# Layer norm statistics of a four-layer graph network: the eps addition and the shift on GpSimd beside the power

## The reference

```
def _layernorm(x, axis=-1, eps=1e-05):
    m = jnp.mean(x, axis=axis, keepdims=True)
    v = jnp.var(x, axis=axis, keepdims=True)
    return (x - m) / jnp.sqrt(v + eps)

x = _layernorm(x + _L0_gnn_ref(x, adj, weight, bias))      # (adj x + x) W + b, each row over its length
x = _layernorm(x + _L1_gnn_ref(x, adj, adj, ..., 5))       # five steps of a gated recurrent unit
x = _layernorm(x + _L2_gnn_ref(x, adj, W, b))              # normalized adjacency, then a linear map
x = _layernorm(x + _L3_gnn_ref(x, adj, W, e, bias))        # attention over adj > 0, softmax, two maps
```

## Time and profile before

| | us |
|---|---|
| median of 3 runs | 800.88 (800.42 to 801.36) |
| the profiled execution | 799.98 |
| its span, first to last instruction | 798.3 |
| PE busy | 770.0 (96%) |
| DVE busy | 651.3 (82%) |
| ACT busy | 515.2 (65%) |
| POOL busy | 117.1 (15%) |

### The profile page before, as it was taken

How to read it: one execution, slowest core, us unless ns; L and a number is a source line. 1 busy time by engine, 2 the same in 40 slices (tenths; PEclk the granted TensorE clock), 3 DMA queues, 4 the chain that set the end, 5 groups by cost and what they waited for, 6 DMA issues and landing times.

```text
span 798.3 us, 12062 instructions
## 1 busy us (share of the span) xinstructions
PE 770.0 (96%) x3822; PEld 638.7 (80%) x3824; DVE 651.3 (82%) x1578; ACT 515.2 (65%) x1050; POOL 117.1 (15%) x127
## 2 busy tenths in 40 slices
PE   7999988899999999999999999999999999999996
PEld 6888766687888888888888888888877787888885
DVE  6788999988877777777778777777999999986444
ACT  4768756678666666666666666666677766665445
POOL 1354422200000000000000000000112133332222
PEclk9999999999999999999999999999999999999998
DMA  6300000100100000000000000000000000000112
GB/s 186 128 1 2 1 0 1 53 1 9 45 1 0 1 1 0 0 0 0 0 0 0 0 0 0 0 1 1 1 1 1 1 2 1 1 0 14 53 54 93
DMA packets 8782, 13.09 MB, mean 16 GB/s; under 512 B 2336, under 2 KB 3872, under 8 KB 8480
## 3 DMA queue, kind: packets, MB, share of 16 engines
q1 hardware_dynamic: 8736, 12.53, 4.6%
HBM read 7.28 MB, written 5.24 MB: 16 GB/s over the span
## 4 chain that ended last, share of the span: by engine, by line
PE 67%; DVE 24%; ACT 5%; issue 2%; DMA 1%; SPq 0%; POOL 0%; ACTq 0%
PE agg_ps L930 11%; PE agg_ps L932 11%; PE agg_ps L931 11%; PE gate_ps L860 5%; PE gate_ps L862 5%; PE gate_ps L861 5%; PE cand_ps L860 3%; PE cand_ps L862 3%; DVE stats L765 3%; PE cand_ps L861 3%; PE turn_ps L969 3%; PE gate_ps L867 3%; PE cand_ps L867 3%; DVE nat_lo L777 2%; DVE cand L733 2%
## 5 line engine op out<-in xcount | busy, mean ns | idle before, releaser
L576 POOL TENSOR_TENSOR rstd<-mean_var,half 128x4 f32<-128x4 f32 x64 | 78.5, 1226 | 570.6 <-DVE mean_var L772 570.5
L930 PE MATMUL agg_ps<-adj_hi,nat_hi 128*128 128x512 f32 x384 | 151.9, 396 | 0.0
L932 PE MATMUL agg_ps<-adj_hi,nat_lo 128*128 128x512 f32 x384 | 150.1, 391 | 0.0
L931 PE MATMUL agg_ps<-adj_lo,nat_hi 128*128 128x512 f32 x384 | 149.6, 390 | 0.0
L462 ACT ACTIVATE reset_hi<-gate_r 128x512 fp32r<-128x512 f32 x80 | 50.6, 632 | 105.2 <-DVE gate_r L741 105.2
L724 DVE TENSOR_TENSOR agg_lo<-agg_ps,agg_hi 128x512 fp32r<-128x512 f32 x80 | 55.1, 689 | 63.6 <-ACT agg_hi L429 63.5
L390 ACT ACTIVATE res<-res,shift,rstd 128x128 f32<-128x128 f32 x210 | 87.9, 484 | 10.1 <-DVE shift L784 10.1
L932 PEld LDWEIGHTS agg_ps<-adj_hi,nat_lo 128*128 128x128 f32 x384 | 72.0, 188 | 16.1
L931 PEld LDWEIGHTS agg_ps<-adj_lo,nat_hi 128*128 128x128 f32 x384 | 72.2, 188 | 15.6
L930 PEld LDWEIGHTS agg_ps<-adj_hi,nat_hi 128*128 128x128 f32 x384 | 72.2, 188 | 15.0
L446 ACT ACTIVATE gate_r<-gate_ps,bias 128x512 f32<-128x512 f32 x80 | 55.1, 689 | 39.4 <-PE gate_ps L862 39.4
(11 more groups left out here) (174 smaller groups left out, 1705.6 us busy)
## 6 DMA issues: line engine op xcount, KB each, us to landing
res<-in_x SPq DMA_DIRECT2D x16, 256.0 KB, 5.5
out<-res SPq DMA_DIRECT2D x16, 256.0 KB, 2.0
rows<-in_adj SPq DMA_DIRECT2D x4, 256.0 KB, 3.9
mix_rows<-feat SPq DMA_DIRECT2D x1, 1024.0 KB, 3.9
later<-mix_rows SPq DMA_DIRECT2D x1, 1024.0 KB, 4.8
gate_z<-in_L_gnn_w_w SPq DMA_DIRECT2D x3, 128.0 KB, 5.4
gate_r<-in_L_gnn_bias SPq DMA_DIRECT2D x2, 64.0 KB, 5.5
gate_z<-in_L_gnn_u_w SPq DMA_DIRECT2D x2, 64.0 KB, 4.6
```

The source lines that it names most:

```text
L576: pool.tensor_tensor(rstd[:, i % RING, :], mean_var[:, i % RING, :, 1], half[:, :], ALU.pow).then_inc(rstd_made, 1)
L930: pe.matmul(ps, nat_hi[:, b, k, :], m_hi[:, k, :], start=(k == 0), stop=False)
L931: pe.matmul(ps, nat_hi[:, b, k, :], m_lo[:, k, :], start=False, stop=False)
L932: last = pe.matmul(ps, nat_lo[:, b, k, :], m_hi[:, k, :], start=False, stop=(k == T - 1))
```

## The change

VectorE no longer adds eps and no longer makes the shift. GpSimd waits for `aggregated` instead of `stats_made` and does four operations on 128 x 4 elements: `shift = -mean`, `var + eps` in place, the power into `rstd`, and, behind a wait for its own power, `shift * rstd`. The first two each go through `link`, which makes GpSimd wait for its own operation. The shift is made in the slot of the statistics, no longer a slot later, and `rstd_made` and `shift_made` both come from GpSimd.

```
--- before.py
+++ after.py
@@ -294,7 +294,7 @@
         state_hi_made = sem("state_hi_made")
         squared, length_made, shift_made = sem("squared"), sem("length_made"), sem("shift_made")
         statted, aggregated = sem("statted"), sem("aggregated")
-        stats_made, rstd_made = sem("stats_made"), sem("rstd_made")
+        rstd_made = sem("rstd_made")
         normed, normed_act = sem("normed"), sem("normed_act")
         split_hi_made, split_lo_made = sem("split_hi_made"), sem("split_lo_made")
         l2_hi_made, l2_lo_made, mix_hi_made = sem("l2_hi_made"), sem("l2_lo_made"), sem("mix_hi_made")
@@ -572,9 +572,14 @@
                         pool.tensor_tensor(r, r, half[:, :], ALU.pow).then_inc(length_made, 1)
                 for n in norms_at(s, "stats"):
                     i = NORMED.index(n)
-                    pool.wait_ge(stats_made, i + 1)
-                    pool.tensor_tensor(rstd[:, i % RING, :], mean_var[:, i % RING, :, 1], half[:, :],
-                                       ALU.pow).then_inc(rstd_made, 1)
+                    pool.wait_ge(aggregated, i + 1)
+                    r = mean_var[:, i % RING, :, 1]
+                    back = shift[:, i % RING, :]
+                    link(pool.tensor_scalar(back, mean_var[:, i % RING, :, 0], -1.0, None, ALU.mult))
+                    link(pool.tensor_scalar(r, r, EPS_LN, None, ALU.add))
+                    pool.tensor_tensor(rstd[:, i % RING, :], r, half[:, :], ALU.pow).then_inc(rstd_made, 1)
+                    pool.wait_ge(rstd_made, i + 1)
+                    pool.tensor_tensor(back, back, rstd[:, i % RING, :], ALU.mult).then_inc(shift_made, 1)
                 k = s - L2_ROWS_AT
                 if 0 <= k < T:
                     pool.wait_ge(turn_read, reads(TURN_NO["d_row", 0]))
@@ -768,9 +773,6 @@
                     for t in range(T):
                         last = dve.bn_aggr(mean_var[:, i % RING, t, :], stats[:, i % 4, t, :])
                     last.then_inc(aggregated, 1)
-                    dve.wait_ge(aggregated, i + 1)
-                    dve.tensor_scalar(mean_var[:, i % RING, :, 1], mean_var[:, i % RING, :, 1], EPS_LN, None,
-                                      ALU.add).then_inc(stats_made, 1)
                 for n in norms_at(s, "split"):
                     if stage(n) != L3:
                         dve.wait_ge(split_hi_made, nth(SPLIT, n))
@@ -778,11 +780,6 @@
                                           nat_hi[:, n % B, :, :].bitcast(F32), ALU.subtract).then_inc(split_lo_made, 1)
                 if s + 3 < B:
                     x_lo(s + 3)
-                for n in norms_at(s, "shift"):
-                    i = NORMED.index(n)
-                    dve.wait_ge(rstd_made, i + 1)
-                    dve.scalar_tensor_tensor(out=shift[:, i % RING, :], in0=mean_var[:, i % RING, :, 0], scalar=-1.0,
-                                             in1=rstd[:, i % RING, :], op0=ALU.mult, op1=ALU.mult).then_inc(shift_made, 1)
                 k = s - ADJ_AT
                 if 0 <= k < T:
                     dve.wait_ge(adj_hi_made, k + 1)
```

More of the change, by code:

```diff
@@ L780, in slot @@
                     x_lo(s + 3)
[L781 to L785, removed]
                 k = s - ADJ_AT
```

## The result

The changed kernel takes 794.61 us (median of 4 runs, 794.53 to 795.43) against 800.65 us (800.22 to 801.36) for the kernel before beside it: ratio 0.9926, 95% interval 0.9909 to 0.9943, 6.04 us less. The profiled execution took 795.43 us with a span of 793.7 us. The forecast was 794.4 us. The total fits; two of its terms don't, and they miss in opposite directions.

What follows compares the result with a forecast made beforehand. VectorE was taken to set the pace only in two stretches, with TensorE holding most of the rest. Terms -1.9 - 4.7 + 0 + 0.1 = -6.5 us, applied to the 800.88 us median, gave 794.4 us; range 790.5 to 799.5.

Steps and rivals of the forecast that it cites:

- Step 1: Eps add and shift removed from VectorE: 0.19 plus 0.07 us, together 0.26 us less per norm.
- Step 2, stretch A: Layer 0's norms overlapping the first recurrent step, slots 16 to 23: seven slots pay 0.265 us each, 1.9 us.
- step 6: GpSimd's 512-wide operations in eight slots start about 1.0 us later and meet other VectorE operations: -4.8 to +1.8 us, taken as zero.
- Step 2, stretch B: Norms of the last recurrent step and first of layer 2: 0.2 + 3.7 + 0.8 = 4.7 us gained.
- Step 3: Added GpSimd operations: about 1.0 us more per norm, some 2.3 us from bn_aggr to shift, and GpSimd keeps up.
- Step 4: GpSimd's wait for its own power, some 0.08 us; the delay queued behind is covered, ScalarE's vanished shift waits count zero.
- Step 5: Port GpSimd shares with VectorE: the three short new operations cost VectorE nothing; bounds zero to about 0.25 us each.
- point 3: The prediction's part on added GpSimd work: about 1.0 us more per norm, with GpSimd keeping up.
- the bound below, -4.8 us: Most that eight slots could gain if VectorE's PSUM-reading operation covered the later 512-wide GpSimd operations.
- Step 7: End of the kernel, last norm's longer GpSimd chain against earlier starts: net +0.1 us, between -0.2 and +0.6.
- stretch A pays nothing: Rival: 512-wide operations fall at their worst (+1.8) and eat the 1.9 us of slots 16 to 23: 796.2 us, chance 0.15.

Runs made afterwards that it cites:

- e2: Changed kernel with the eps addition given back to VectorE, so only the shift moves to GpSimd: 798.92 us.
- e4: Changed kernel with three more 128x4 GpSimd multiplies per norm behind the last one, products unread: 793.87 us.
- e5: Changed kernel with one more 256-wide GpSimd multiply per norm in slots 85 to 95, products unread: 800.13 us.
- e1_eps_only: Changed kernel with the shift given back to VectorE, so only the eps addition moves to GpSimd: 792.69 us.
- e11: Changed kernel with layer 0's shift back on VectorE, the other shifts on GpSimd, and the four 512-wide additions in slots 4 to 7: 789.64 us.
- e10: Changed kernel with only the eps addition on GpSimd and the four 512-wide additions in slots 4 to 7: 790.03 us.

## Why the prediction was right, and where it was not

**What bounds the kernel.** Right. The gain is in the two stretches where VectorE worked nearly all the time and nowhere else: from 701.8 us of before to the end the lead is the same within 0.02 us at 19 of 21 norms, and at the other two VectorE is a little further ahead of TensorE.

**Step 1, 0.265 us per norm.** Slightly small: 0.29 us in stretch B, 0.22 for eps and 0.07 for the shift. The distance to nat_lo fell from 0.49 to 0.29 us, as said; the missing 0.02 us is nat_lo itself, 0.66 us instead of 0.69, so that what follows starts sooner.

**Step 2, stretch A 1.9 us.** Wrong: 0.8 us. Slots 20 to 23 gave 0.18 to 0.22 each, slots 16, 18 and 19 gave 0.22, 0.10 and 0.28, together 1.39 instead of 7 x 0.265, and slot 17 cost 0.57. The prediction had slot 17 right in that VectorE waits there for the length and gains nothing, but took that for zero. The trace of after has the reason: nat_lo comes 0.2 us sooner after bn_aggr and now falls on the length's power (1.54 instead of 1.0 us), for which VectorE itself is waiting; e2, where nat_lo stays behind the power, loses none of it. So 1.04 us less than forecast: 0.57 in slot 17 and 0.47 in the seven others, where the stops by the wide operations grew (step 6).

**Step 2, stretch B 4.7 us.** Mechanism right, size 5.25 us. The 14 norms give 3.98 us instead of 3.7 (mostly 0.29 for 0.265 us each, 0.22 in two of them). The three slots without a split gave 0.04, 0.10 and 0.11 us, 0.24 together where 0.2 was taken, and what follows the 14 norms 1.03 us instead of 0.8. TensorE has no wait left between 560 and 700 us, where it had 1.7 and 0.7 us. That VectorE's further gain becomes idle time is seen as well: at the norm of 688.79 us of before it is 5.70 us ahead of its old time, and two norms later 4.60 (+0.58, +0.52), where TensorE sets the pace.

**Step 3, GpSimd 1.0 us more per norm, hidden.** 0.76 us more busy, and it is hidden. From bn_aggr to the shift it is 616.96 - 614.15 = 2.8 us, not 2.3, because the first operation waits behind nat_lo. In slot 20, for which step 6 had taken about 3 us, it is 3.3.

**Step 4, the new wait.** Harmless, as said: GpSimd's power and last multiply follow one another at their usual 0.08 us. But what is queued behind it is not harmless in slots 16 to 23; that is step 6. ScalarE's 10.1 us of waits went and were worth nothing, as counted: e2 removes them and gains 2.15 us, which the VectorE instructions explain.

**Step 5, the port.** Right in its main point, by the earlier trace rows against the rule: small operations cost VectorE 0.03 us or nothing (e4), a wide one nearly its length (e5). The Trainium skill (SBUF — State Buffer, section "SBUF: two separate sides") has the first comer hold the port pair for its whole instruction; the runs agree with it for 256 and 512 columns, to within 0.17 us, and for the power on 128 x 4 elements they do not: L734, with two SBUF inputs, begins 0.63 us into the 1.04 us of power and takes its usual 0.68 us. What I left out is the other direction. "The GpSimd operations may each wait up to 0.6 us, harmless by point 3" is false where somebody waits for them: that is slot 17, and it is also how the wide operations came to start 3.27 us after bn_aggr.

**Step 6, the 512-wide operations, taken as zero.** In slots 18 to 23 they did move from L718 to the state's second step (L738, L733 of before), one of the three places that the prediction named, and in slot 20 the stop was 1.13 instead of 1.05 us. Over the eight slots the stops grew by 0.7 us, which is the larger part of what stretch A lacks besides slot 17's late length. And the bound below, -4.8 us, was not idle: in e1_eps_only, where the operation starts 1.1 us sooner than in the kernel after, the stop is 0.40 us shorter than before in slot 20, and the eight slots sum to -2.8 us. (By that bound the time is 794.4 - 4.8 = 789.6 us; the prediction's 790.5 has no working of its own.) Had the change moved the eps alone, these steps would have given 7 x 0.19 + 0.2 + 14 x 0.19 + 0.7 = 4.9 us, and it gave 8.4.

**Step 7, the tail +0.1 us.** ScalarE's last work, of the kernel after:

```profile
788.32 1.65 ACT L390 ACTIVATE res<-res,shift,rstd 128x128 f32<-128x128 f32 x4 [0.94 <-POOL shift L582]
790.36 0.88 ACT L390 ACTIVATE res<-res,shift,rstd 128x128 f32<-128x128 f32 x2 [0.39 <-POOL shift L582]
```

It begins 793.34 - 788.32 = 5.02 us sooner than in the earlier trace rows, 0.42 more than the lead of 4.60, for the shift of the norm before last comes that much sooner; then it waits 0.39 us for the last shift. It ends at 791.24 against 795.76, 4.52 us sooner: +0.08 us. Right.

**What the profile was to show.** 0.30 us from bn_aggr to nat_lo (0.29), the two waits of TensorE (gone), the pairs at 0.60 us with a long L738 behind (so). The slots of stretch B are 7.01, not 7.05 us. VectorE's busy time fell by 14.6 us, not 20: the 20 was the sum of 64 x (0.17 + 0.15) us, though step 1 had just said that VectorE's instructions overlap. In the slot shown, busy time fell from 7.09 to 6.81, 0.28 us, and elsewhere by less.

The gain was forecast at 6.5 us and came out at 6.04: stretch B gave 0.55 us more and stretch A 1.1 us less. The total of 794.4 came nearer still to 794.61 us because the kernel before took 800.65 us beside it and not 800.88. That the errors of the two stretches cancel by half is luck, and the rival "stretch A pays nothing" (796.2) was closer to the 0.8 us of stretch A than the forecast of 1.9 was; of its longer stops, taken at 1.8 us, 0.7 were there, and the rest of the loss is the late length, which it did not have.

Not settled: what in the power leaves VectorE alone, its width or something else in it, since no other long and narrow operation was run; and whether e11 is faster than e10 by the 0.4 us of the medians.

## What to carry to other kernels

When small operations are moved to another engine's queue, the first thing to price is what stands behind them there: here a few tenths of a microsecond on VectorE were the direct gain, and when the 512-wide GpSimd operation began decided as much again, so that one part of the change was faster than all of it. Parts of a change that shift a start do not add; a ledger of one slot, with saved instructions in one column and the length of the stop in the other, does. And an operation that may be slowed harmlessly is harmless only in the slots where nobody waits for it, so each slot with a wait for that engine has to be looked at by itself.

## What the runs showed of the hardware that was not expected

- A GpSimd multiply or addition that begins first holds a VectorE operation on two SBUF tiles for its own length less 0.16 or 0.17 us: 0.03 us for 128 x 4 (0.19 us long), 0.57 us for 128 x 256 (0.74 us long), 1.13 us for 128 x 512 (1.29 us long). A power on 128 x 4, 1.04 us long, doesn't hold it. A VectorE operation that reads PSUM (agg_lo) runs beside a wide one in its usual 0.68 us.
- The other way round a GpSimd operation suffers when VectorE comes first: 0.58 us instead of 0.24 for a small one beside a subtraction of two SBUF tiles, a power 1.54 instead of 1.04 us, or 1.32 beside a one-input tensor_scalar on feat. Which of two starts 0.01 to 0.06 us apart comes first decides it.
- Between two dependent operations, GpSimd needs about 0.08 us (615.20 to 615.28, 615.51 to 615.59), so a short chain of them costs little more than its parts.
